# Attention kernel of two layers: both head groups averaged in one block, the row maxima turned in one 16-column turn, VectorE's and ScalarE's work put at other steps

## Chip, core, metric

One core of a Trainium2 chip. The metric is the device time of one execution in microseconds, lower is better.

## The reference, cut to what matters

Two layers of the same form run over x (128 rows of 256 tokens, 256 channels). Within a layer the rows are independent of each other; group norm needs all of them.

```python
def layer(x):                       # 128 rows x 256 tokens x 256 channels
    n = group_norm(x)
    q, k, v = heads(n @ Wq.T) * 32**-0.5, heads(n @ Wk.T), heads(n @ Wv.T)   # 8 heads of 32
    w = softmax(q @ k.T + bias + mask_bias)     # 256 x 256 for each row and head
    avg = sigmoid(n @ Wg.T + gate_bias) * (w @ v)
    return x + avg @ Wo.T + bo
```

## The kernel before

Each engine has one program: for each layer it goes through slots s = -2 to 132, one for each of the 128 rows and some to fill and drain; slots 8 to 123 are in a hardware loop of four slots a turn. In slot s the engines work on several rows at once: the projections are those of row s, the maxima those of row s-1, the exponentials of rows s-2 and s-3, the average of row s-3 or s-4, the output of row s-5. No planner decides anything: each engine executes its instructions in the order of the code, and an instruction whose semaphore isn't there holds all that stand behind it on its engine. TensorE and VectorE divide a slot into eight steps. In each step TensorE computes the logits of one head for the maxima (`max_bank`, two banks in turn) and of one head for the exponentials (`exp_bank`, two banks), and VectorE takes them: `maxima` (two halves, bias added, row maximum taken) and `logits` (bias added, written to `probs`).

Between these stands the rest. On TensorE before: step 0 `average(r, 1)` of row s-4; step 1 `maxima_rows`, the turn of the row maxima into `proj_b` (L757), and the q projection into `proj_a`; step 2 the k projection into `proj_b`; step 3 the output; step 4 the gate projection into `proj_b`; step 5 `average(r, 0)` of row s-3; steps 6 and 7 the v projection. `average` sums probabilities times v into `av_bank` (L739) and the sums of probabilities into `den_bank` (L746), in f32.

The row maxima are subtracted as two f16 rows of `q_stack`: ScalarE writes `coarse` (L463) from the turned maxima in `proj_b`, VectorE writes `fine` (L637) from `coarse` and `proj_b`, and SyncE sends both into the stack. The k projection writes over the same `proj_b`, so it waits for `fine`:

```python
if step == 2 and s.active():
    wait(pe, gate_ready, s.plus(-1).count(1, 1))
    wait(pe, fine_ready, s.plus(-2).count(1, 1))
    project(s, 1, pb, 0, None)
```

ScalarE's `split` takes a projection out of PSUM twice, as `k_hi` (f16, L444) and `k_f` (f32, L445); GpSimd makes `k_lo` of them; SyncE's queue sends, in this order, `coarse`, `fine`, `q_hi` twice, `k_hi` twice, `q_lo` and `k_lo` into the stacks, each when its semaphore is there. Step 0 of the next slot waits for all of them (`stack_in`), and the gate projection waits for `k_f`. VectorE's `gated_average`, `turn_denominator`, `invert` and `turn_reciprocal` prepare the gated, normalised average of row s-4.

Of the kernel before, what the change touches and what calls it, by code (L numbers as in the profile page):

```python
# [34 lines left out]
P = 128  # L35
# [78 lines left out]
def build(nc, a, out):  # L114
# [10 lines left out]
    with ctx:  # L125
# [71 lines left out]
        shift_ps = pb[0:HEADS, 0, :]  # L197
# [147 lines left out]
        def _(pool):  # L345
# [9 lines left out]
            def slot(s):  # L355
# [8 lines left out]
                if r.active():  # L364
                    key_sum(r, 0)
                if s.active():
                    low_half(s, 0)
                    low_half(s, 1)
                r = s.plus(-5)
                if r.active():  # L370
                    i = r.ring(2)
                    wait(pool, res_in[i], r.lap(2, 16, 16))
                    wait(pool, out_left, r.count(1, 1), pool_passed)
                    pool.tensor_tensor(y[:, i], y[:, i], attn[:, i], ALU.add).then_inc(y_ready, 1)  # L374
                r = s.plus(-4)
# [6 lines left out]
                r = s.plus(-3)  # L382
                if r.active():
                    key_sum(r, 1)
                r = s.plus(1)
                if r.active():
                    i = r.ring(2)
                    wait(pool, x_norm_ready, r.count(1, 1))
                    wait(pool, g_psum, r.plus(-2).count(1, 1))
                    wait(pool, v_psum, r.plus(-2).count(1, 1))  # L390
                    wait(pool, x_hi_ready, r.count(1, 1), pool_passed)
                    pool.tensor_tensor(x_lo[:, i], x_norm[:, i], x_hi[:, i], ALU.subtract).then_inc(x_lo_ready, 1)  # L392
# [10 lines left out]
            def key_sum(r, g):  # L403
                wait(pool, probs_ready, r.count(4, 2 * g + 2), pool_passed)
                wait(pool, den_psum, r.plus(-1).count(2, g + 1), pool_passed)
                pr = probs[:, r.ring(2), 4 * g:4 * (g + 1)]
                pool.tensor_tensor(probs_sum[:, g], pr[:, :, 0, :], pr[:, :, 1, :], ALU.add).then_inc(sum_ready, 1)  # L407
# [6 lines left out]
        def _(act):  # L414
# [32 lines left out]
            def slot(s):  # L447
# [9 lines left out]
                r = s.plus(-2)  # L457
                if r.active():
                    i = r.ring(2)
                    act.wait_ge(shift_psum, r.count(1, 1))  # L460
                    q = r.plus(-2)
                    wait(act, shift_in[q.ring(4)], shift_full(q))
                    act.activation(coarse[:, i], shift_ps, ACT.Copy, scale=-FINE / COARSE).then_inc(coarse_ready, 1)  # L463
# [10 lines left out]
                if s.active():  # L474
                    split(s, 0)
                    split(s, 1)
                r = s.plus(1)
                if r.active():
# [9 lines left out]
                    op.then_inc(x_norm_ready, 1)  # L488
                r = s.plus(-5)
# [8 lines left out]
                r = s.plus(-3)  # L498
                if r.active():
                    exponentials(r, 1, [0, 1])  # L500
# [9 lines left out]
                r = s.plus(1)  # L510
                if r.active():
                    i = r.ring(2)
                    act.wait_ge(x_norm_ready, r.count(1, 1))
                    wait(act, g_psum, r.plus(-2).count(1, 1))
                    wait(act, v_psum, r.plus(-2).count(1, 1))
                    act.activation(x_hi[:, i], x_norm[:, i], ACT.Copy).then_inc(x_hi_ready, 1)  # L516
# [5 lines left out]
                r = s.plus(-4)  # L522
                if r.active():
                    b = r.ring(2)
                    act.wait_ge(gated_ready, r.count(1, 1))
                    wait(act, out_psum, r.plus(-2).count(1, 1))
                    act.activation(gated_hi[:, b], gated[:, b], ACT.Copy).then_inc(gated_hi_ready, 1)  # L527
                if s.active():
                    act.wait_ge(v_psum, s.count(1, 1))
                    wait(act, av_psum, s.plus(-4).count(2, 2))  # L530
                    act.activation(v_sb[:, s.ring(4)], pa[:, :, :], ACT.Copy, scale=V_SCALE / W_SCALE).then_inc(v_ready, 1)  # L531
# [17 lines left out]
        def _(dve):  # L549
# [59 lines left out]
            def maxima(r, h):  # L609
# [6 lines left out]
                for t in range(TT):  # L616
# [3 lines left out]
                                                  op0=ALU.add, op1=ALU.max, accum_out=row_max[:, i, t, place(h):place(h) + 1])  # L620
                op.then_inc(max_done, 1)

            def logits(r, h):
# [3 lines left out]
                if h % 4 == 0:  # L627

                    wait(dve, av_psum, r.plus(-2).count(2, h // 4 + 1))
                    wait(dve, sum_ready, r.plus(-2).count(2, h // 4 + 1))  # L630
# [9 lines left out]
            def gated_average(r):  # L640
                dve.wait_ge(av_psum, r.count(2, 2))
# [5 lines left out]
            def turn_denominator(r):  # L647
                dve.wait_ge(den_psum, r.count(2, 2))
# [13 lines left out]
            def slot(s):  # L662
                l = s.layer
                for step in range(8):
                    if s.plus(-1).active():
                        maxima(s.plus(-1), step)
                    if step == 3 and s.plus(-4).active():
                        turn_denominator(s.plus(-4))
# [15 lines left out]
                    if step in (6, 7) and l == 0 and r.active():  # L684
                        dve.wait_ge(y_ready, r.count(1, 1))
                        c = step - 6
                        op = dve.bn_stats(stats[:, c, bass.ds(r.index(), 1), :], y[:, r.ring(2), c])  # L687
                        if c == CT - 1:
                            op.then_inc(stats_ready, 1)
# [7 lines left out]
        def _(pe):  # L697
# [33 lines left out]
            def average(r, g):  # L731
                pe.wait_ge(probs_ready, r.count(4, 2 * g + 2))
                pe.wait_ge(v_ready, r.count(1, 1))
                if g == 0:
                    wait(pe, avg_ready, r.plus(-1).count(1, 1))
                for t in range(TT):
                    for j in range(4):
                        h = 4 * g + j
                        op = pe.matmul(av_bank[HC * j:HC * (j + 1), g, :], v_sb[:, r.ring(4), t, HC * h:HC * (h + 1)],  # L739
                                       probs[:, r.ring(2), h, t, :], start=(t == 0), stop=(t == TT - 1))  # L740
                op.then_inc(av_psum, 1)
                pe.wait_ge(sum_ready, r.count(2, g + 1))
                if g == 0:
                    wait(pe, den_left, r.plus(-1).count(1, 1))
                for j in range(4):
                    op = pe.matmul(den_bank[HC * j:HC * (j + 1), g, :], ones[:, :], probs_sum[:, g, j, :],  # L746
                                   start=True, stop=True)
                op.then_inc(den_psum, 1)

            def maxima_rows(r):  # L750
# [5 lines left out]
                for t in range(TT):  # L756
                    op = pe.transpose(shift_ps[:, t * P:(t + 1) * P], row_max[:, i, t], ident[:, :])  # L757
                op.then_inc(shift_psum, 1)
# [12 lines left out]
            def slot(s):  # L771
                for step in range(8):
# [16 lines left out]
                    if step == 0 and r.active():  # L789
                        average(r, 1)  # L790
# [25 lines left out]
                    r = s.plus(-3)  # L816
                    if step == 5 and r.active():
                        average(r, 0)
# [63 lines left out]
```

## Time and profile before

| | |
|---|---|
| median of 3 runs | 3749.67 us (3744.16 to 3749.84) |
| the profiled execution | 3750.91 us, its span 3749.0 us |
| TensorE busy | 3495.1 us, 93% |
| VectorE busy | 3539.6 us, 94% |
| ScalarE, GpSimd busy | 73%, 81% |
| granted TensorE clock | 0.991 in the mean |

The span holds a prologue of some 150 us (the statistics of the input), the 128 rows of layer 0, a short boundary, and the 128 rows of layer 1. A busy share says how long an engine had an instruction in it, not which engine sets the pace; that is read from the waits and the chain.

### The profile page before, as it was taken

How to read it: one execution, taken by the hardware profiler on the slowest of the kernel's cores; microseconds unless marked ns; L12 is line 12 of the kernel's file. 1: busy time of each engine (PE TensorE's matmuls, PEld its weight loads, DVE VectorE, ACT ScalarE, POOL GpSimd, SP SyncE). 2: the span in 40 equal slices, each digit the busy share in tenths (PEclk: the TensorE clock that was granted, in tenths of full speed). 3: DMA queues.
4: the chain of work that ended last, by engine and by line, in shares of the span. 5: the costliest groups of instructions: out<-in, count | busy, mean ns of one | idle time of the engine just before them, and what ended most of it. 6: DMA issues, size and time to landing. Idle time of an engine off the chain costs nothing.

```text
span 3749.0 us, 121609 instructions
## 1 busy us (share of the span) xinstructions
PE 3495.1 (93%) x36360; PEld 2630.4 (70%) x36360; DVE 3539.6 (94%) x11937; ACT 2742.8 (73%) x4625; POOL 3021.8 (81%) x2056
## 2 busy tenths in 40 slices
PE   0499999999999999999968999999999999999997
PEld 0377777777777777777746777777777777777775
DVE  6599999999999999999968999999999999999997
ACT  0377777777777777777746777777787777777775
POOL 1288888888888888888856888888888888888887
PEclk9999999999999999999979999999999999999998
DMA  8555555555555555555534555555555555555553
GB/s 321 173 112 118 113 112 114 115 115 113 115 113 117 113 113 112 118 113 112 114 107 107 119 118 116 120 117 118 120 119 117 117 118 117 119 116 119 120 118 75
DMA packets 450644, 454.08 MB, mean 121 GB/s; under 512 B 42880, under 2 KB 445440, under 8 KB 445968
## 3 DMA queue, kind: packets, MB, share of 16 engines
q1 hardware_dynamic: 241680, 251.85, 35.5%
q10 hardware_dynamic: 208896, 201.38, 19.5%
q8 instruction: 37, 0.61, 0.1%
q14 instruction: 31, 0.25, 0.0%
HBM read 182.39 MB, written 67.24 MB: 67 GB/s over the span
## 4 chain that ended last, share of the span: by engine, by line
PE 58%; DVE 25%; issue 11%; DMA 3%; DVEq 1%; POOL 1%; SPq 1%; ACT 0%; POOLq 0%; ACTq 0%
PE proj_b L712 15%; DVE max_bank L618 10%; PE proj_a L712 9%; PE proj_a L766 9%; PE max_bank L723 8%; PE av_bank L739 7%; PE exp_bank L728 7%; DVE probs L631 6%; PE den_bank L746 3%; DVE row_max L618 3%; DVE stats L687 2%; DMA bias_k<-in_xT 1%; DVE recip L658 1%; DVE fine L637 1%; PE proj_b L757 1%
## 5 line engine op out<-in xcount | busy, mean ns | idle before, releaser
L618 DVE CUSTOM_DVE_ANT_0 max_bank<-max_bank,bias_q 128x256 f32<-128x256 f32 x4096 | 1637.6, 441 | 127.7 <-PE max_bank L723 95.7
L407 POOL TENSOR_TENSOR probs_sum<-probs 128x1024 f32<-128x1024 f32 x512 | 1207.8, 2359 | 308.3 <-ACT probs L434 154.3
L631 DVE TENSOR_TENSOR probs<-exp_bank,bias_k 128x512 f32<-128x512 f32 x2048 | 1390.0, 679 | 7.4 <-PE exp_bank L728 7.4
L723 PE MATMUL max_bank<-k_stack,q_stack 96*128 96x256 f16 (+1 forms) x4096 | 788.5, 274 | 11.8 <-DMA k_stack<-k_lo 9.9
L728 PE MATMUL exp_bank<-q_stack,k_stack 100*128 100x256 f16 x4096 | 784.4, 272 | 8.8 <-DVE probs L631 6.5
L431 ACT ACTIVATE probs<-probs,mask_bias 128x1024 f32<-128x1024 f32 x512 | 573.0, 1149 | 61.4 <-DVE probs L631 61.3
L434 ACT ACTIVATE probs<-probs 128x1024 f32<-128x1024 f32 x512 | 525.7, 1056 | 91.9 <-DVE probs L631 91.8
L618 DVE DVE_READ_ACCUMULATOR2_ANT row_max<- 128x1 f32 x4096 | 568.0, 139 | 0.0
L739 PE MATMUL av_bank<-probs,v_sb 128*32 128x256 f32 x8192 | 550.1, 386 | 3.0 <-ACT probs L431 1.6
L723 PEld LDWEIGHTS max_bank<-k_stack,q_stack 96*128 96x128 f16 (+1 forms) x4096 | 381.5, 98 | 164.0 <-DVE row_max L618 103.5
L728 PEld LDWEIGHTS exp_bank<-q_stack,k_stack 100*128 100x128 f16 x4096 | 395.1, 97 | 71.9 <-DVE probs L631 12.4
L392 POOL TENSOR_TENSOR x_lo<-x_norm,x_hi 128x512 f16<-128x512 f32 x256 | 299.0, 1168 | 147.0 <-ACT x_hi L516 147.0
L380 POOL TENSOR_TENSOR gated<-avg,recip 128x512 f32<-128x512 f32 x256 | 327.9, 1281 | 110.1 <-DVE recip L658 81.7
L374 POOL TENSOR_TENSOR y<-y,attn 128x512 f32<-128x512 f32 x256 | 327.1, 1278 | 101.1 <-ACT attn L495 65.3
L531 ACT ACTIVATE v_sb<-proj_a 128x512 f32<-128x512 f32 x256 | 152.9, 597 | 289.8 <-PE proj_a L712 289.8
L739 PEld LDWEIGHTS av_bank<-probs,v_sb 128*32 128x32 f32 x8192 | 214.0, 109 | 200.5 <-issue 57.6
L444 ACT ACTIVATE k_hi<-proj_b 128x512 f16<-128x512 f32 x256 | 152.8, 597 | 245.6 <-PE proj_b L712 245.6
L746 PE MATMUL den_bank<-probs_sum,ones 128*32 128x256 f32 x4096 | 317.7, 382 | 5.3 <-POOL probs_sum L407 5.3
L400 POOL TENSOR_TENSOR k_lo<-k_f,k_hi 128x512 f16<-128x512 f32 x256 | 296.9, 1160 | 29.5 <-issue 18.1
L400 POOL TENSOR_TENSOR q_lo<-q_f,q_hi 128x512 f16<-128x512 f32 x256 | 296.5, 1158 | 26.2 <-ACT q_f L445 26.2
L361 POOL TENSOR_TENSOR gated_lo<-gated,gated_hi 128x512 f16<-128x512 f32 x256 | 297.8, 1163 | 1.6 <-ACT gated_hi L527 1.6
L486 ACT ACTIVATE x_norm<-x_in,shift_x,rstd 128x256 f32<-128x256 f32 x512 | 278.5, 599 | 7.0 <-DMA x_in<-in_xT 6.8
(120 smaller groups left out, 6919.1 us busy)
## 6 DMA issues: line engine op xcount, KB each, us to landing
q_stack<-q_hi SPq DMA_DIRECT2D x512, 128.0 KB
k_stack<-k_hi SPq DMA_DIRECT2D x512, 128.0 KB
x_in<-in_xT ACTq DMA_DIRECT2D x128, 256.0 KB, 2.7
q_stack<-q_lo SPq DMA_DIRECT2D x256, 128.0 KB
k_stack<-k_lo SPq DMA_DIRECT2D x256, 128.0 KB
y<-in_xT ACTq DMA_DIRECT2D x128, 256.0 KB, 3.0
layer_out<-y ACTq DMA_DIRECT2D x128, 256.0 KB, 2.7
x_in<-layer_out ACTq DMA_DIRECT2D x128, 256.0 KB, 2.7
```

The costliest lines, as they stand in the source:

```text
L400: pool.tensor_tensor(qk_lo[m][:, b], qk_f32[m][:, b], qk_hi[m][:, b], ALU.subtract).then_inc(qk_lo_ready[m], 1)
L407: pool.tensor_tensor(probs_sum[:, g], pr[:, :, 0, :], pr[:, :, 1, :], ALU.add).then_inc(sum_ready, 1)
L431: act.activation(pr, pr, ACT.Exp, bias=mask_bias[:, bass.ds(r.index(), 1), t]).then_inc(probs_ready, 1)
L434: act.activation(pr, pr, ACT.Exp).then_inc(probs_ready, 1)
L618: op = dve.tensor_tensor_reduce(out=max_bank[h % 2][:, t, :], in0=max_bank[h % 2][:, t, :], in1=bias_q[:, h, t, :], scale=1.0 / FINE, scal ...
L631: dve.tensor_tensor(probs[:, r.ring(2), h], exp_bank[h % 2][:, :, :], bias_k[:, h], ALU.add).then_inc(logits_ready, 1)
L712: op = pe.matmul(ps[:, tile, :], lhs, rhs, start=(n == 0), stop=(n == len(terms) - 1))
L723: op = pe.matmul(bank_[:, t, :], q[0:n, t * P:(t + 1) * P], k[0:n, :], start=True, stop=True)
L728: op = pe.matmul(bank_[:, t, :], k[0:n, t * P:(t + 1) * P], q[0:n, :], start=True, stop=True)
L739: op = pe.matmul(av_bank[HC * j:HC * (j + 1), g, :], v_sb[:, r.ring(4), t, HC * h:HC * (h + 1)], probs[:, r.ring(2), h, t, :], start=(t == ...
L746: op = pe.matmul(den_bank[HC * j:HC * (j + 1), g, :], ones[:, :], probs_sum[:, g, j, :], start=True, stop=True)
L766: op = pe.matmul(pa[:, o, :], w[l][:, e, o * P:(o + 1) * P], g[:, b, e, :], start=(n == 0), stop=(n == len(terms) - 1))
```

## The change

Four things are put differently. TensorE averages both head groups in one block at step 0, both for row s-4, with the eight groups of `av_bank` first and the denominators behind them. The row maxima are stored as (head, half) so that one turn of 16 columns replaces two of 8; `coarse` and `fine` become 16 x 128 instead of 8 x 256. VectorE's `fine` moves from step 1 to step 2, the gated average from 2 to 4, the turn of the denominator and its reciprocal from 3 to 5, the turn of the reciprocal from 4 to 6, and both `bn_stats` to step 7. ScalarE's order is written anew: among others the first exponentials of the second head group now stand between the split of q and the split of k. GpSimd's order is written anew too.

```diff
-        row_max = sb("row_max", [P, 2, TT, HEADS], f32)
-        coarse = sb("coarse", [HEADS, 2, TOK], f16)
-        fine = sb("fine", [HEADS, 2, TOK], f16)
+        row_max = sb("row_max", [P, 2, HEADS, TT], f32)
+        coarse = sb("coarse", [HEADS * TT, 2, P], f16)
+        fine = sb("fine", [HEADS * TT, 2, P], f16)
-        shift_ps = pb[0:HEADS, 0, :]
+        shift_ps = pb[0:HEADS * TT, 0, 0:P]
...
                 if s.active():
                     split(s, 0)
-                    split(s, 1)
+                r = s.plus(-3)
+                if r.active():
+                    exponentials(r, 1, [0])
+                if s.active():
+                    split(s, 1)
+                r = s.plus(-3)
+                if r.active():
+                    exponentials(r, 1, [1])
...
-                r = s.plus(-3)
-                if r.active():
-                    exponentials(r, 1, [0, 1])
...
-                    if step == 3 and s.plus(-4).active():
+                    if step == 5 and s.plus(-4).active():
                         turn_denominator(s.plus(-4))
...
-                    if step == 1 and s.plus(-2).active():
+                    if step == 2 and s.plus(-2).active():
                         fine_shift(s.plus(-2))
...
-                        if step == 2:
+                        if step == 4:
                             gated_average(r)
-                        if step == 3:
+                        if step == 5:
                             invert(r)
-                        if step == 4:
+                        if step == 6:
                             turn_reciprocal(r)
...
+            def average(r):
+                pe.wait_ge(probs_ready, r.count(4, 4))
                 pe.wait_ge(v_ready, r.count(1, 1))
+                wait(pe, avg_ready, r.plus(-1).count(1, 1))
+                for g in range(HG):
+                    for t in range(TT):
+                        for j in range(4):
+                            h = 4 * g + j
+                            op = pe.matmul(av_bank[HC * j:HC * (j + 1), g, :],
...
+                op.then_inc(av_psum, 1)
+                wait(pe, den_left, r.plus(-1).count(1, 1))
+                for g in range(HG):
+                    pe.wait_ge(sum_ready, r.count(2, g + 1))
...
-                for t in range(TT):
-                    op = pe.transpose(shift_ps[:, t * P:(t + 1) * P], row_max[:, i, t], ident[:, :])
-                op.then_inc(shift_psum, 1)
+                pe.transpose(shift_ps, row_max[:, i].rearrange("p h t -> p (h t)"), ident[:, :]
+                             ).then_inc(shift_psum, 1)
...
                     if step == 0 and r.active():
-                        average(r, 1)
+                        average(r)
...
-                    if step == 5 and r.active():
-                        average(r, 0)
```

On VectorE, steps 1 and 2 of a slot before (the `ISA` rows are the two halves of `maxima`, L631 is `logits`):

```order
L618 ISA max_bank,row_max<-max_bank,bias_q 128x256 [waits max_psum]
L618 ISA row_max 128x1
L618 ISA max_bank,row_max<-max_bank,bias_q 128x256
L618 ISA row_max 128x1
L631 TENSOR_TENSOR probs<-exp_bank,bias_k 128x512 [waits exp_psum]
L637 SCALAR_TENSOR_TENSOR fine<-coarse,proj_b 8x256 [waits coarse_ready]
L618 ISA max_bank,row_max<-max_bank,bias_q 128x256 [waits max_psum]
```

And the same two steps of the changed kernel, in which each line number is one higher:

```order
L632 TENSOR_TENSOR probs<-exp_bank,bias_k 128x512 [waits exp_psum]
L619 ISA max_bank,row_max<-max_bank,bias_q 128x256 [waits max_psum]
L619 ISA row_max 128x1
L619 ISA max_bank,row_max<-max_bank,bias_q 128x256
L619 ISA row_max 128x1
L632 TENSOR_TENSOR probs<-exp_bank,bias_k 128x512 [waits exp_psum]
L638 SCALAR_TENSOR_TENSOR fine<-coarse,proj_b 16x128 [waits coarse_ready]
```

`fine` now stands behind the maxima and the logits of step 2, which wait for TensorE's matmuls of step 2.

On TensorE, step 0 and the start of step 1 before:

```order
L723 MATMUL max_bank<-k_stack,q_stack 128x256 [waits max_done,stack_in1]
L723 MATMUL max_bank<-k_stack,q_stack 128x256
L728 MATMUL exp_bank<-q_stack,k_stack 128x256 [waits logits_ready]
L728 MATMUL exp_bank<-q_stack,k_stack 128x256
L739 MATMUL av_bank<-probs,v_sb 32x256 [waits v_ready,probs_ready]
L739 MATMUL av_bank<-probs,v_sb 32x256 x7
L746 MATMUL den_bank<-probs_sum,ones 32x256 [waits sum_ready]
L746 MATMUL den_bank<-probs_sum,ones 32x256 x3
L757 MATMUL proj_b<-ident,row_max 8x128 [waits fine_ready,gate_ready,max_done]
L757 MATMUL proj_b<-ident,row_max 8x128
```

The same place in the changed kernel, and below the break the end of its step 2, where the k projection still waits for `fine_ready`:

```order
L739 MATMUL av_bank<-probs,v_sb 32x256 [waits avg_ready,v_ready,probs_ready]
L739 MATMUL av_bank<-probs,v_sb 32x256 x15
L747 MATMUL den_bank<-probs_sum,ones 32x256 [waits sum_ready,den_left]
L747 MATMUL den_bank<-probs_sum,ones 32x256 x3
L747 MATMUL den_bank<-probs_sum,ones 32x256 [waits sum_ready]
L747 MATMUL den_bank<-probs_sum,ones 32x256 x3
L757 MATMUL proj_b<-ident,row_max 16x128 [waits fine_ready,gate_ready,max_done]
...
L728 MATMUL exp_bank<-q_stack,k_stack 128x256
L712 MATMUL proj_b<-x_hi,w_hi0k 128x256 [waits fine_ready,gate_ready]
```

The block at step 0 holds twice the matmuls, the turn is one instruction, and what the k projection waits for is as it was.

On ScalarE, from the split of q to the second exponentials before (L434 is `exponentials`, L486 and L495 are x_norm and the output's bias):

```order
L444 ACTIVATE q_hi<-proj_a 128x512 [waits q_lo_ready,stack_in1,q_psum]
L445 ACTIVATE q_f<-proj_a 128x512
L444 ACTIVATE k_hi<-proj_b 128x512 [waits k_lo_ready,stack_in1,k_psum]
L445 ACTIVATE k_f<-proj_b 128x512
L486 ACTIVATE x_norm<-x_in,shift_x,rstd 128x256 [waits x_loaded0,x_lo_ready]
L486 ACTIVATE x_norm<-x_in,shift_x,rstd 128x256
L495 ACTIVATE attn<-proj_a,out_bias 128x256 [waits y_ready,out_psum]
L495 ACTIVATE attn<-proj_a,out_bias 128x256
L434 ACTIVATE probs<-probs 128x4x256 [waits logits_ready]
```

The same place in the changed kernel:

```order
L444 ACTIVATE q_hi<-proj_a 128x512 [waits q_lo_ready,stack_in1,q_psum]
L445 ACTIVATE q_f<-proj_a 128x512
L434 ACTIVATE probs<-probs 128x4x256 [waits logits_ready]
L444 ACTIVATE k_hi<-proj_b 128x512 [waits k_lo_ready,stack_in1,k_psum]
L445 ACTIVATE k_f<-proj_b 128x512
L434 ACTIVATE probs<-probs 128x4x256
```

The exponentials, which wait for VectorE's logits of step 3, now stand ahead of `k_hi` and `k_f`.

## Rows read from the trace of the kernel before

**Rows 1.** Page, part 1: busy time, share of the span, instructions of each engine.

```profile
PE 3495.1 (93%) x36360; PEld 2630.4 (70%) x36360; DVE 3539.6 (94%) x11937; ACT 2742.8 (73%) x4625; POOL 3021.8 (81%) x2056
```

**Rows 2.** Timeline, one slot of layer 0: start us, us, engine, what, [idle before].

```profile
1000.24 0.38 PE L757 MATMUL proj_b<-ident,row_max 128*8 128x128 f32 x2
...
1002.01 0.69 DVE L631 TENSOR_TENSOR probs<-exp_bank,bias_k 128x512 f32<-128x512 f32 x1
...
1002.61 0.40 DVE L637 SCALAR_TENSOR_TENSOR fine<-coarse,proj_b 8x256 f16<-8x256 f16 x1
...
1003.16 0.38 PE L712 MATMUL proj_b<-x_hi,w_hi0k 128*128 128x256 f16 x2 [0.34 <-DVE fine L637]
...
1004.46 0.38 PE L723 MATMUL max_bank<-k_stack,q_stack 96*128 96x256 f16 x2
...
1004.66 0.60 ACT L444 ACTIVATE k_hi<-proj_b 128x512 f16<-128x512 f32 x1 [1.17 <-PE proj_b L712]
...
1005.04 0.43 DVE L618 CUSTOM_DVE_ANT_0 max_bank<-max_bank,bias_q 128x256 f32<-128x256 f32 x1
...
1005.16 0.59 ACT L445 ACTIVATE k_f<-proj_b 128x512 f32<-128x512 f32 x1
...
1005.37 1.19 SPq L326 DMA_DIRECT2D k_stack<-k_hi  x2
...
1005.77 0.71 DVE L649 STREAM_TRANSPOSE den_turned<-den_bank 128x512 f32<-128x512 f32 x1
...
1007.37 0.55 SPq L326 DMA_DIRECT2D k_stack<-k_lo  x1
...
1009.07 0.40 DVE L618 CUSTOM_DVE_ANT_0 max_bank<-max_bank,bias_q 128x256 f32<-128x256 f32 x1
...
1012.14 0.38 PE L723 MATMUL max_bank<-k_stack,q_stack 96*128 96x256 f16 x2
...
1014.10 0.09 PEld L757 LDWEIGHTS proj_b<-ident,row_max 128*8 128x8 f32 x2 [0.41 <-issue]
```

**Rows 3.** Critical chain in order of time, layer 1: start us, us, what.

```profile
2603.38 1.31 PE proj_b L712 x12
...
2605.13 1.00 PE av_bank L739 x16
2606.13 0.43 PE den_bank L746 x8
2606.56 0.33 PE max_bank L723 x2
...
2610.74 0.31 PE proj_b L757 x2
...
2624.29 0.31 PE proj_b L757 x2
```

**Rows 4.** Groups by line: busy us, mean ns of one, idle before.

```profile
L431 ACT ACTIVATE probs<-probs,mask_bias 128x1024 f32<-128x1024 f32 x512 | 573.0, 1149 | 61.4 <-DVE probs L631 61.3
...
L434 ACT ACTIVATE probs<-probs 128x1024 f32<-128x1024 f32 x512 | 525.7, 1056 | 91.9 <-DVE probs L631 91.8
...
L687 DVE BATCH_NORM_STATS2 stats<-y 128x256 f32 (+1 forms) x256 | 106.2, 416 | 11.7 <-POOL y L374 11.7
L637 DVE SCALAR_TENSOR_TENSOR fine<-coarse,proj_b 8x256 f16<-8x256 f16 x256 | 102.0, 398 | 0.0
...
L599 DVE TENSOR_TENSOR centred<-centred 128x2 f32<-128x2 f32 x2 | 0.3, 160 | 0.0
```

**Rows 5.** Timeline, where PE waited for the last stack transfer: start of layer 0.

```profile
156.46 0.60 SPq L326 DMA_DIRECT2D k_stack<-k_lo  x1
...
160.03 0.39 PE L723 MATMUL max_bank<-k_stack,q_stack 96*128 96x256 f16 x2 [1.21 <-DMA k_stack<-k_lo]
```

**Rows 6.** Critical chain in order of time, layer 0: start us, us, what.

```profile
1016.56 0.33 DVE fine L637
```

**Rows 7.** Windows between the layers: busy of each engine, PEclk is the granted clock.

```profile
1940.00:1945.00 5.00, 2.48 (x12) 1.66 (x12) 0.00 (x0) 0.63 (x1) 1.57 (x2) 0.50 0.15 52
1970.00:1975.00 5.00, 2.79 (x24) 2.27 (x24) 0.00 (x0) 3.12 (x7) 2.31 (x2) 1.00 0.65 140
```

More of the change, by code:

```diff
@@ L456, in slot @@
                     act.dma_start(x_in[:, i], channel_major(src[l], r.index() * TOK, TOK)).then_inc(x_loaded[i], 16)
-                r = s.plus(-2)
+                r = s.plus(-5)
                 if r.active():
[L459 to L463, printed above, removed]
+                    b = r.ring(2)
+                    act.wait_ge(gated_ready, r.count(1, 1))
+                    wait(act, out_psum, r.plus(-2).count(1, 1))
+                    act.activation(gated_hi[:, b], gated[:, b], ACT.Copy).then_inc(gated_hi_ready, 1)
                 r = s.plus(-3)
@@ L473, in slot @@
                     act.dma_start(y[:, i], channel_major(src[l], r.index() * TOK, TOK)).then_inc(res_in[i], 16)
-                if s.active():
-                    split(s, 0)
-                    split(s, 1)
+                r = s.plus(-2)
+                if r.active():
+                    i = r.ring(2)
+                    act.wait_ge(shift_psum, r.count(1, 1))
+                    q = r.plus(-2)
+                    wait(act, shift_in[q.ring(4)], shift_full(q))
+                    act.activation(coarse[:, i], shift_ps, ACT.Copy, scale=-FINE / COARSE).then_inc(coarse_ready, 1)
                 r = s.plus(1)
@@ L488, in slot @@
                     op.then_inc(x_norm_ready, 1)
+                    act.wait_ge(x_norm_ready, r.count(1, 1))
+                    wait(act, g_psum, r.plus(-2).count(1, 1))
+                    wait(act, v_psum, r.plus(-2).count(1, 1))
+                    act.activation(x_hi[:, i], x_norm[:, i], ACT.Copy).then_inc(x_hi_ready, 1)
+                if s.active():
+                    split(s, 0)
+                r = s.plus(-3)
+                if r.active():
+                    exponentials(r, 1, [0])
+                if s.active():
+                    split(s, 1)
+                r = s.plus(-3)
+                if r.active():
+                    exponentials(r, 1, [1])
                 r = s.plus(-5)
@@ L627, in logits @@
                 if h % 4 == 0:
-                    wait(dve, av_psum, r.plus(-2).count(2, h // 4 + 1))
+                    wait(dve, av_psum, r.plus(-2).count(1, 1))
                     wait(dve, sum_ready, r.plus(-2).count(2, h // 4 + 1))
@@ L676, in slot @@
                     if r.active():
[L677 removed]
+                        if step == 4:
                             gated_average(r)
[L679 removed]
+                        if step == 5:
                             invert(r)
[L681 removed]
+                        if step == 6:
                             turn_reciprocal(r)
                     r = s.plus(-5)
[L684 removed]
+                    if step == 7 and l == 0 and r.active():
                         dve.wait_ge(y_ready, r.count(1, 1))
[L686 to L689, printed above, removed]
+                        for c in range(CT):
+                            op = dve.bn_stats(stats[:, c, bass.ds(r.index(), 1), :], y[:, r.ring(2), c])
+                        op.then_inc(stats_ready, 1)
             for l in range(2):
```

62 lines of the change are left out of this document (17 added, 45 removed).

## Prediction

> **What bounds the kernel now.** I read the page first: VectorE is busy 94% and TensorE 93% of the span [rows 1], so neither busy share settles it, and a change that makes one wait for the other has no spare time to hide in. Then I read the timeline of one slot. The reader is to see two turns of the row maxima, 13.86 us apart (1014.10 - 1000.24) [rows 2]: that is a slot in layer 0. In layer 1 the chain in order of time has them 13.55 us apart (2624.29 - 2610.74), and its pieces join end to end on TensorE [rows 3]. With 128 rows a layer the slots are 128 x (13.86 + 13.55) = 3508 us of the span; the rest is prologue and boundary. So the question is how long one slot takes afterwards.
>
> The coupling that matters is small at present. The k projection waits for `fine`, and TensorE loses 0.34 us by it: `fine` starts at 1002.61, takes 0.40, and the projection starts 0.15 after its end, at 1003.16 [rows 2]. It is that little because VectorE does `fine` after the logits of step 1, while TensorE still has a whole q projection ahead of its step 2.
>
> **What the change saves.** A block of eight groups and their denominators is 1.00 + 0.43 us, and the maxima behind it take 0.33, where 1.31 for twelve matmuls says that two should take 0.22 [rows 3]. Since 8 denominator instructions are 0.43, the 16 others should be 0.86: 0.14 goes into entering the block and 0.11 into leaving it. One block in place of two saves 0.25 us of TensorE, one turn in place of two 0.10 (half of 0.31 less the 0.11 for leaving). On VectorE `fine` goes from 398 ns at 256 elements towards the 160 ns of an operation of 2 elements; in proportion 128 elements take 0.28 us. The bounds are 0.16 and 0.40 [rows 4]. I take 0.28. If nothing new had to be waited for, the slot would shorten by 0.12 us in layer 0 (VectorE) and by 0.35 in layer 1 (TensorE), 60 us in all.
>
> **What it adds: three legs, walked through from step 0.** I put t = 0 at TensorE's first matmul of step 0, layer 0.
>
> TensorE: maxima and exponentials' logits 0.44; the merged block 2 x 1.43 - 0.14 = 2.72, so 3.16; leaving it and one turn 0.21, so 3.37; the logits of step 1 0.44, the q projection 1.31; step 2 starts at 5.12 [rows 3].
>
> VectorE starts a head's maxima 0.58 us after TensorE's first matmul for it (1004.46 to 1005.04), needs 0.73 for them (to 1005.77), and starts what follows the logits 0.60 behind their start (1002.01 to 1002.61) [rows 2]. So the maxima of step 2 start at 5.70, the logits at 6.43, `fine` at 7.03, it ends at 7.31, and the k projection starts at 7.46. TensorE was ready at 5.56: it now stands 1.9 us, since nothing but those logits lies between what VectorE needs and what it holds back. That is the first new stall. The range of `fine` moves it by 0.12 at most.
>
> The k projection takes 1.30 (1003.16 to 1004.46) [rows 2]; step 3 starts at 8.76, VectorE's maxima at 9.34, its logits at 10.07, done 0.69 later at 10.76. Only then can ScalarE start the exponentials that now stand ahead of the split of k: 10.86 with 0.1 to hand over, as SyncE takes between the end of `k_hi` (1005.26) and its issue at 1005.37. They take 1.06 [rows 4] of which the next instruction overlaps 0.1, as `k_f` starts 0.50 into a `k_hi` of 0.60 [rows 2]: `k_hi` starts at 11.81 and ends at 12.41. Before, it followed its projection at once. `k_f` ends at 12.90 (start 0.50 later, 0.59 long), and the gate projection, ready at 8.76 + 0.44 + 1.31 + 0.44 = 10.95, waits for it until 13.0: the second new stall, 2.0 us.
>
> SyncE issues `k_hi` at 12.52 and, 2.00 later as before (1005.37 to 1007.37), `k_lo` at 14.52 [rows 2]. Where TensorE was seen to wait for this transfer, it started 3.57 us after the issue (156.46 to 160.03) [rows 5]; in the steady part it needed no wait 4.77 us after it (1007.37 to 1012.14) [rows 2], which is the bound from above. I take 3.7, near the one that shows the landing. Then step 0 of the next slot starts at 18.2. TensorE, with 1.31 + 3 x 0.44 + 2 x 0.66 behind 13.0, is ready at 16.95: the third stall, 1.3 us. In layer 1 the exponentials are 0.09 longer (1149 against 1056 ns) [rows 4]: 18.3.
>
> The Trainium skill ("DMA: Bandwidth & Descriptors", section "Anatomy of one DMA") fits one DMA of the GpSimd path with a fixed 2.0 us and its bytes over 436 GB/s. By that the last 128 KB would be there 2.3 us after issue, at an estimated 16.8, and the transfer would not bind; the trace shows 3.57 us with five others ahead of it, so the sum goes by the trace.
>
> The sum: 128 x (18.2 - 13.86) = 555 and 128 x (18.3 - 13.55) = 608, together 1163 us on the profiled 3750.91, which is within 0.04% of the median of 3749.67: 4914, and I say **4910 us**. VectorE's moved turns and ScalarE's other moves cost nothing beside this: both engines stand for several microseconds a slot. That cover is thin on VectorE in layer 0 only, next.
>
> **The rivals.**
>
> *The transfer does not bind (0.13).* Then the loop closes through an engine. TensorE's gives 16.95 and 17.05. VectorE's: maxima of step 5 start at 13.0 + 1.31 + 0.58 = 14.9; before, from those maxima (1009.07) to the next `fine` (1016.56) it took 7.49 [rows 2, 6]; now two turns (0.71 each [rows 2], less an overlap of 0.08 as others have), the reciprocal (0.16, that of the smallest operation [rows 4]) and step 2's maxima and logits (1.33) stand in that stretch too, while some 0.2 of waiting for TensorE may drop out. `fine` comes at 24.9 against 7.03, a slot of 17.9. In layer 1 it goes without the two `bn_stats` (0.42 each [rows 4], less the overlap) and waits 0.1 longer for ScalarE, 17.3. Time: 3751 + 128 x (4.04 + 3.75) = 4750. For it speaks that transfers find less traffic in a longer slot; against it, that 3.57 was seen in the thin traffic of the first slots.
>
> *The transfer lands late (0.06).* With the full 4.77 a slot is 1.07 longer: 3751 + 1163 + 274 = 5190. `coarse` and `fine` are twice as many packets of half the size; they have 2 us of room before step 4 needs them.
>
> *Only one stall comes (0.04).* If ScalarE found the logits of step 3 done, k would leave PSUM at once and only the wait for `fine` stayed: TensorE's 13.4 us of a slot before (13.55 less some 0.2 for `fine`), less 0.35, plus 1.9 is 14.9, so 4060 us. It decides if VectorE runs a step ahead of TensorE; but its logits need TensorE's step 3.
>
> *The clock falls (0.03).* TensorE works 13 of 18.2 us, with gaps of 1.3 to 2 us. Between the layers the granted clock was 0.50, the 1.2 GHz level, in 5 us in which TensorE was busy for 2.48, and 1.00, 2.4 GHz, in 5 us with 2.79 [rows 7]. At the low level the parts of the loop on TensorE, 5.12 + 1.30, would double: 24.6 and 24.7 a slot, 3751 + 128 x (10.8 + 11.1) = 6550. The Trainium skill ("TensorE: Matmul & The Clock Gate", section "HAM oscillation — how this bites in real kernels") describes kernels in which waits between bursts bring the clock down each time; the row at 1.00 with 2.79 busy, less than TensorE has in every stretch of the new slot but the longest gap, speaks against it here.
>
> *Faster (0.02).* If TensorE kept its pace past `fine`, the savings alone would remain: 3751 - 60 = 3690. That needs `fine` done by t = 5.56 rather than 7.31. The point from which the change is a gain is a loop below 13.86: all three stalls, 5.2 us together, would have to shrink to 0.5.
>
> **How the numbers follow.** My case (0.72) has its own range of 4800 to 5020: hand-overs of 0.1 us and the landing by -0.3 to +0.4 us, 256 times. The range of 8 in 10 takes in rival one and part of the late landing: 4700 to 5060. A change within 0.2% is about what a measurement of this kernel cannot tell from none: every case but the last is slower by far (0.98); I leave 0.01 of it for no change: faster 0.02, same 0.01, slower 0.97.
>
> **What the profile will show.** The turns (L757) 18.2 and 18.3 us apart; TensorE's waits for `fine` before the k projection near 1.9 us, for `k_f` before the gate projection near 2 us, for the stack's transfer near 1.3 us, each some 250 times; ScalarE idle before the first exponentials of group 1, `k_hi` right behind them. TensorE's busy share falls to about 70%; `fine` takes some 280 ns. I am wrong if the k projection starts less than 1.5 us behind step 2's logits, if `k_hi` does not follow an exponential, or if the clock is below 0.97.

## The result and the profile after

The changed kernel takes 4987.35 us (median, 4966.6 to 4993.02), beside 3749.47 for the kernel before on the same chip: a ratio of 1.3296 [1.3265, 1.3326]. 4910 was forecast, so it is inside the range and 77 us above the number. The profiled execution took 4993.02 us with a span of 4990.5.

The page of the kernel after, part 1, and two rows of its part 5, answer to [rows 1, 4]:

```profile
PE 3730.6 (75%) x36104; PEld 2667.7 (53%) x36104; DVE 3543.4 (71%) x11937; ACT 2714.5 (54%) x4625; POOL 3020.0 (61%) x2056
...
L431 ACT ACTIVATE probs<-probs,mask_bias 128x1024 f32<-128x1024 f32 x512 | 585.3, 1144 | 633.6 <-DVE probs L632 633.6
L434 ACT ACTIVATE probs<-probs 128x1024 f32<-128x1024 f32 x512 | 538.7, 1053 | 655.4 <-DVE probs L632 655.4
```

VectorE's and ScalarE's busy times are those of before to within 30 us; both only wait more. TensorE has 256 matmuls fewer and is busy for 236 us more. a_fine1 below does the same matmuls at a clock of 0.990 and is busy for 3581.7 us, so about 150 of the 236 us go with the lower clock here; the rest was not taken apart. The exponentials now have 634 and 655 us of idle time ahead of them where [rows 4] had 61 and 92: ScalarE comes to them before the logits exist.

The view of the waits of the kernel after (who waits, for whom; us in total, times, longest):

```profile
PE proj_b L712 <- ACT k_f L445: 474.9, 256, 3.0
PE proj_b L712 <- DVE fine L638: 424.6, 252, 2.0
...
PEld exp_bank L728 <- DVE probs L632: 258.9, 466, 1.7
...
PE exp_bank L728 <- DVE probs L632: 135.2, 270, 1.4
...
PE max_bank L723 <- DMA k_stack<-k_lo: 15.7, 24, 2.4
```

Two of the three forecast stalls are there with the forecast count. The third is not: the stack's transfer is named 24 times, and `exp_bank` waiting for VectorE's logits some 270 times stands in its place. The transfer is not out of the loop, though: in the chain that ended last (part 4 of the page, shares of the span) it has 8%.

```profile
PE proj_b L712 14%; PE av_bank L739 10%; PE proj_a L712 8%; DMA k_stack<-k_lo 8%; DVE max_bank L619 8%; DVE probs L632 7%; PE max_bank L723 6%; PE den_bank L747 4%; PE exp_bank L728 4%; ACT k_hi L444 3%; DVE row_max L619 3%; ACT k_f L445 2%; POOL k_lo L400 1%; DVE den_turned L650 1%; PE proj_b L757 1%
```

The timeline of one slot of layer 0 (idle time before in brackets) shows all of it, and answers to [rows 2]:

```profile
1008.41 0.28 PE L757 MATMUL proj_b<-ident,row_max 128*16 128x128 f32 x1
...
1010.28 0.38 PE L723 MATMUL max_bank<-k_stack,q_stack 96*128 96x256 f16 x2
...
1011.58 0.68 DVE L632 TENSOR_TENSOR probs<-exp_bank,bias_k 128x512 f32<-128x512 f32 x1
...
1012.19 0.27 DVE L638 SCALAR_TENSOR_TENSOR fine<-coarse,proj_b 16x128 f16<-16x128 f16 x1
...
1012.51 0.39 PE L712 MATMUL proj_b<-x_hi,w_hi0k 128*128 128x256 f16 x2 [1.63 <-DVE fine L638]
...
1015.13 0.68 DVE L632 TENSOR_TENSOR probs<-exp_bank,bias_k 128x512 f32<-128x512 f32 x1
...
1015.94 1.06 ACT L434 ACTIVATE probs<-probs 128x1024 f32<-128x1024 f32 x1 [3.30 <-DVE probs L632]
...
1016.90 0.58 ACT L444 ACTIVATE k_hi<-proj_b 128x512 f16<-128x512 f32 x1
...
1018.02 0.39 PE L712 MATMUL proj_b<-x_hi,w_hi0g 128*128 128x256 f16 x2 [1.83 <-ACT k_f L445]
...
1019.58 0.55 SPq L326 DMA_DIRECT2D k_stack<-k_lo  x1
...
1020.65 0.71 DVE L650 STREAM_TRANSPOSE den_turned<-den_bank 128x512 f32<-128x512 f32 x1
...
1020.88 0.38 PE L723 MATMUL max_bank<-k_stack,q_stack 96*128 96x256 f16 x2
...
1021.29 0.65 DVE L632 TENSOR_TENSOR probs<-exp_bank,bias_k 128x512 f32<-128x512 f32 x1
...
1022.00 0.39 PE L728 MATMUL exp_bank<-q_stack,k_stack 100*128 100x256 f16 x2 [0.73 <-DVE probs L632]
...
1023.15 0.39 PE L723 MATMUL max_bank<-k_stack,q_stack 96*128 96x256 f16 x2
...
1023.46 0.11 PEld L728 LDWEIGHTS exp_bank<-q_stack,k_stack 100*128 100x128 f16 x2 [0.20 <-DVE probs L632]
```

- `fine` lasts 0.27 us and stands behind the logits of step 2; the k projection stands 1.63 us.
- ScalarE waits 3.30 us for the logits of step 3, does an exponential, and only then `k_hi`. The gate projection stands 1.83 us.
- From the issue of `k_lo` (1019.58) to step 0 (1023.15) it is 3.57 us, the very figure of [rows 5]. Yet TensorE had already lost time in step 7: its logits started at 1022.00, 0.90 after the maxima's two matmuls (0.22) were through, because VectorE turned the denominator before it did the logits of step 5. Only 0.26 is lost at 1023.15 (the projection's last pair starts at 1022.67 and takes 0.22), and the weight load for the next logits still waits for VectorE at 1023.46. So two legs end together at step 0. The maxima wait for the transfer, as I read it: VectorE had left their bank 0.29 before (1022.86), and in a_qlo below, where the transfer leaves earlier, TensorE starts 0.05 behind VectorE there (1002.71 to 1002.76). The logits, 0.31 later, wait for VectorE. In 226 of 228 steady slots TensorE's logits of step 0 start within 0.1 us of the end of VectorE's logits of step 6.

In the chain this turn is at 1008.48 and the next at 1026.58, 18.10 us on. At full clock the slots are 18.18 us in layer 0 and 18.26 in layer 1, where 18.2 and 18.3 were forecast. But not all slots have the full clock. The windows of the kernel after put two gate projections side by side, the first starting at 998.74 and the second at 1018.02 (length; busy of PE, PEld, DVE, ACT, POOL; granted clock; DMA share, GB/s):

```profile
995.60:999.10 3.50, 1.66 (x16) 1.24 (x15) 2.94 (x10) 2.45 (x4) 0.05 (x1) 0.99 0.13 40
999.10:1002.50 3.40, 3.40 (x19) 2.34 (x17) 0.68 (x3) 2.09 (x5) 3.09 (x3) 0.50 0.76 154
1002.50:1006.00 3.50, 3.09 (x30) 1.92 (x32) 3.50 (x12) 0.60 (x1) 1.59 (x1) 1.00 0.22 76
1014.90:1018.40 3.50, 1.67 (x16) 1.25 (x15) 2.93 (x9) 2.46 (x4) 0.07 (x1) 1.00 0.15 43
1018.40:1021.80 3.40, 2.86 (x27) 2.23 (x24) 1.88 (x6) 2.06 (x5) 3.09 (x3) 1.00 0.75 154
```

TensorE did the same before both, 1.66 and 1.67 us of work in 3.5. Behind the first the granted clock is 0.50, the 1.2 GHz level, for 3.4 us and TensorE is busy all of it; behind the second it stays at 1.00, 2.4 GHz. Of 114 steady slots of layer 0 that I went through 48 have such a stretch, in layer 1 55 of 115, and such a slot takes 19.1 to 19.2 us. Each stretch begins 0.07 to 1.27 us behind the gate projection's start, in this kernel never at the k projection. 103 slots by about 0.95 us are some 98 us.

### The profile page after: what moved, and what is told of

Same layout as the page of the kernel before. It is cut to its first block, busy times and chain, and to the rows that moved or that the text cites. A ratio compares the mean times of both kernels' runs of the same rounds, so it can differ in the third digit from the quotient of the medians.

```text
span 4990.5 us, 119942 instructions
## 1 busy us (share of the span) xinstructions
PE 3730.6 (75%) x36104; PEld 2667.7 (53%) x36104; DVE 3543.4 (71%) x11937; ACT 2714.5 (54%) x4625; POOL 3020.0 (61%) x2056
## 4 chain that ended last, share of the span: by engine, by line
PE 48%; DVE 22%; issue 12%; DMA 9%; ACT 6%; POOL 2%; SPq 1%; DVEq 1%; ACTq 0%; POOLq 0%
PE proj_b L712 14%; PE av_bank L739 10%; PE proj_a L712 8%; DMA k_stack<-k_lo 8%; DVE max_bank L619 8%; DVE probs L632 7%; PE max_bank L723 6%; PE den_bank L747 4%; PE exp_bank L728 4%; ACT k_hi L444 3%; DVE row_max L619 3%; ACT k_f L445 2%; POOL k_lo L400 1%; DVE den_turned L650 1%; PE proj_b L757 1%
## 5 line engine op out<-in xcount | busy, mean ns | idle before, releaser
L728 PE MATMUL exp_bank<-q_stack,k_stack 100*128 100x256 f16 x4096 | 836.8, 288 | 146.1 <-DVE probs L632 135.2
L431 ACT ACTIVATE probs<-probs,mask_bias 128x1024 f32<-128x1024 f32 x512 | 585.3, 1144 | 633.6 <-DVE probs L632 633.6
L434 ACT ACTIVATE probs<-probs 128x1024 f32<-128x1024 f32 x512 | 538.7, 1053 | 655.4 <-DVE probs L632 655.4
L723 PE MATMUL max_bank<-k_stack,q_stack 96*128 96x256 f16 (+1 forms) x4096 | 840.1, 289 | 32.2 <-DMA k_stack<-k_lo 15.7
L728 PEld LDWEIGHTS exp_bank<-q_stack,k_stack 100*128 100x128 f16 x4096 | 378.9, 102 | 334.1 <-DVE probs L632 258.9
L739 PE MATMUL av_bank<-probs,v_sb 128*32 128x256 f32 x8192 | 503.4, 387 | 3.2 <-ACT probs L431 1.7
L723 PEld LDWEIGHTS max_bank<-k_stack,q_stack 96*128 96x128 f16 (+1 forms) x4096 | 398.9, 104 | 160.1 <-DVE row_max L619 58.8
L739 PEld LDWEIGHTS av_bank<-probs,v_sb 128*32 128x32 f32 x8192 | 242.3, 111 | 194.1 <-issue 61.0
L712 PE MATMUL proj_b<-x_hi,w_hi1g 128*128 128x256 f16 x512 | 109.6, 299 | 245.0 <-ACT k_f L445 245.0
L712 PE MATMUL proj_b<-x_hi,w_hi0g 128*128 128x256 f16 x512 | 110.6, 302 | 229.9 <-ACT k_f L445 229.9
```

The source lines that it names most:

```text
L431: act.activation(pr, pr, ACT.Exp, bias=mask_bias[:, bass.ds(r.index(), 1), t]).then_inc(probs_ready, 1)
L434: act.activation(pr, pr, ACT.Exp).then_inc(probs_ready, 1)
L712: op = pe.matmul(ps[:, tile, :], lhs, rhs, start=(n == 0), stop=(n == len(terms) - 1))
L723: op = pe.matmul(bank_[:, t, :], q[0:n, t * P:(t + 1) * P], k[0:n, :], start=True, stop=True)
L728: op = pe.matmul(bank_[:, t, :], k[0:n, t * P:(t + 1) * P], q[0:n, :], start=True, stop=True)
```

## The experiments

**One part undone at a time.** Three kernels from the one after: `fine` at step 1 again; the split of k ahead of the exponentials again; both.

```
a_fine1:   -  if step == 2 and s.plus(-2).active():      # fine_shift
           +  if step == 1 and s.plus(-2).active():
a_ksplit:  -  split(s, 0); exponentials(r, 1, [0]); split(s, 1); exponentials(r, 1, [1])
           +  split(s, 0); split(s, 1); exponentials(r, 1, [0, 1])
a_both:    both edits
```

> The changed kernel with one line put back: VectorE's fine at step 1 again. My theory (each stall is a leg of one loop): TensorE's stall before the k projection (1.63 us in the profile after) goes, everything behind it comes earlier, a slot falls from 18.2 to about 16.5 us, the time to about 4500 us (4450 to 4560). Rival (ScalarE's order or the merged block alone sets the pace, and fine only fills a gap that is there anyway): the time stays above 4900 us.

Measured: 4447.97 us (one execution), 2 below the range, clock 0.990, slots of 16.44 us in layer 0 and 16.51 in layer 1.

> The changed kernel with ScalarE's split of k put back ahead of the exponentials of group 1; all else as changed. My theory: k_hi follows its projection at once, TensorE's stall before the gate projection (1.83 us) goes, and the stack's last transfer leaves some 2 us earlier; a slot of 16.2 to 16.5 us, 4400 to 4500 us. Rival (the wait for fine alone sets the pace): above 4900 us.

Measured: 4413.82 us (one execution), clock 0.990, slots of 16.32 us in both layers.

> The changed kernel with both put back, fine at step 1 and the split of k ahead of the exponentials. If the two waits are all that is wrong, what the change saves should show: 13.4 us a slot, about 3690 us. My theory now is that it does not get there: ScalarE still does x_norm and x_hi ahead of the split of q, so the stack's transfers leave late, and the block of 48 matmuls keeps VectorE waiting: 15.0 to 15.2 us a slot, about 4110 us (4000 to 4200).

Measured: 4036.20 us (one execution), clock 0.991, slots of 14.69 and 14.98, in the range though the slots are shorter than expected.

The waits of the three kernels, in this order, show that each edit takes away its own stall and leaves the other as it was (in the last two the lines of the code stand four lower):

```profile
PE proj_b L712 <- ACT k_f L445: 411.7, 255, 3.0
```

```profile
PE proj_b L708 <- DVE fine L634: 424.8, 252, 2.0
```

```profile
PE proj_b L708 <- ACT k_f L445: 5.4, 9, 1.2
```

So the two stalls are shown, each caused by its own edit. Each kernel is 539 and 574 us faster than the kernel after. In both figures the low clock goes too (92 us, below), so they can't be added: with both stalls gone it is 951 us. The remaining 287 us over the kernel before belong to what is left in a_both: the merged block, the turn, VectorE's moved steps and ScalarE's and GpSimd's other moves. My sum had the block inside TensorE's leg (2.72 us) and put no price on the rest.

**The same parts made alone in the kernel before.**

```
b_fine2:      -  if step == 1 and s.plus(-2).active():   # fine_shift
              +  if step == 2 and s.plus(-2).active():
b_exp_first:  -  split(s, 0); split(s, 1); exponentials(r, 1, [0, 1])
              +  split(s, 0); exponentials(r, 1, [0]); split(s, 1); exponentials(r, 1, [1])
b_merge:      -  average(r, 1) at step 0, average(r, 0) at step 5
              +  average(r) at step 0: both groups' matmuls, then both groups' denominators
b_turn16:     -  row_max [P, 2, TT, HEADS];  two transposes, of row_max[:, i, t]
              +  row_max [P, 2, HEADS, TT];  one transpose, of row_max[:, i] as "p (h t)"
              -  coarse, fine [HEADS, 2, TOK]
              +  coarse, fine [HEADS * TT, 2, P]
```

> The kernel before with one thing of the change alone: VectorE's fine at step 2. My theory: the k projection must wait for the logits of step 2 here as well, 1.5 to 1.7 us more a slot on TensorE: 15.1 to 15.4 us, 4080 to 4180 us. Rival (only behind the merged block is TensorE at step 2 so early that it must wait): below 3800 us.

Measured: 4169.94 us (one execution; before on the same chip 3746.96), clock 0.991, slots of 15.36, as expected. Eight of its steady slots (5 of layer 0, 3 of layer 1) take some 17.0 us and have a stretch of 3.4 us at 0.50. Here it begins at the k projection, 0.9 to 1.1 us behind its start and behind 1.85 us of idle time. A window of b_fine2 behind the k projection that starts at 267.67 (columns as above):

```profile
268.60:271.90 3.30, 3.30 (x17) 2.29 (x16) 1.69 (x6) 2.06 (x4) 1.12 (x2) 0.50 0.32 105
```

> The kernel before with one thing of the change alone: ScalarE's first exponentials of group 1 ahead of the split of k. My theory: k_hi comes some 2 us later, which TensorE waits for before the gate projection and again for the stacks at step 0: 16.3 to 16.5 us a slot, 4400 to 4450 us. Rival (in the old order the exponentials' logits are done in time): below 3800 us.

Measured: 4595.32 us (one execution), 145 to 195 more than expected, and the clock says why: 0.949. Its slots are 16.47 and 16.31 us at full clock and 17.97 and 17.82 with a stretch at 0.50, which 46 of 114 and 58 of 115 have. Those 104 by 1.5 us are 156: without them about 4440, as expected. The waits of b_exp_first:

```profile
PE proj_b L716 <- ACT k_f L445: 630.2, 256, 3.7
```

That is 2.46 us each time, the longest regular wait of any kernel here, and it stands at the gate projection again.

> The kernel before with one thing of the change alone: both groups averaged in one block of 48 matmuls at step 0, VectorE, ScalarE and GpSimd in their old order. By the entering and leaving that it saves on TensorE (0.25 us a slot) it should give 3690 to 3750 us. My theory is that VectorE waits 2.8 us for the next maxima behind the block and that this is not made up: about 14.4 us a slot, 3900 to 3960 us.

Measured: 3920.55 us (one execution), slots of 14.40 and 14.38. The merged block, which by the prediction's estimate TensorE does 0.25 us faster than two, costs 174 us in the old order. The timeline of b_merge shows the reason:

```profile
1001.45 1.93 PE L739 MATMUL av_bank<-probs,v_sb 128*32 128x256 f32 x32
...
1003.68 0.69 DVE L631 TENSOR_TENSOR probs<-exp_bank,bias_k 128x512 f32<-128x512 f32 x1
...
1004.39 0.38 PE L723 MATMUL max_bank<-k_stack,q_stack 96*128 96x256 f16 x2
...
1004.97 0.43 DVE L618 CUSTOM_DVE_ANT_0 max_bank<-max_bank,bias_q 128x256 f32<-128x256 f32 x1 [0.60 <-PE max_bank L723]
```

For the 2.7 us of the block TensorE hands VectorE nothing, VectorE runs dry: it waits for the maxima's matmuls for 287.3 us over the run, 268 times, where the kernel before has 95.7 us, 147 times. These 192 us more are about what the kernel loses. That a VectorE that was 94% busy [rows 1] can't make them up later, while two blocks of half the length find it with work left, is my reading; no run varies the length of the block.

> The kernel before with one part of the change alone: row_max as (head, half), one turn of 16 columns, coarse and fine as 16 x 128. My theory: fine takes 0.27 instead of 0.40 us on VectorE, ScalarE's coarse 0.1 less, TensorE has one turn less (0.11): a slot shorter by 0.12 to 0.15 us in layer 0 and 0.15 to 0.25 in layer 1, together 3700 to 3720 us, a ratio of 0.988 to 0.992. Rival (the stacks' 256-byte pieces land later, or another engine has the pace): 3750 us or more.

Measured: 3703.62 us (median of four executions, 3702.65 to 3708.18), ratio 0.9884 [0.9868, 0.9901], slots of 13.71 and 13.37. This one part of the change is a gain, of 44.5 us or 1.2%, and this kernel beats both. Its groups by line, against 398 ns in [rows 4] for the same values laid out 8 x 256:

```profile
L637 DVE SCALAR_TENSOR_TENSOR fine<-coarse,proj_b 16x128 f16<-16x128 f16 x256 | 67.9, 265 | 0.0
```

`coarse` on ScalarE goes from 361 to 251 ns in the same way. The values are as many; only those of one partition are half as many, and the time falls with them.

**The clock.** Useless work for TensorE in one gap or the other, in scratch space that the program overwrites before it reads it.

```
a_fill:      step 2, ahead of the wait for fine:
             +  for n in range(12): pe.matmul(pb[64:128, 1, :], 64x256 ...)
a_fill_out:  step 3, ahead of output(r, 0):
             +  for n in range(12): pe.matmul(pa[:, n % 2, :], 128x256 ...)
```

> The changed kernel with twelve matmuls without use (64 x 256, f16, 0.109 us each, 1.31 us in all) on TensorE in step 2 ahead of the wait for fine, into a part of proj_b that the k projection writes over afterwards. They fit into the stall of 1.63 us, so the loop stays as long as it was. Theory of the clock: in the profile after, some 4 slots in 10 have 3.4 us at the 1.2 GHz level and are 19.2 instead of 18.2 us; with the longest gap filled TensorE keeps 2.4 GHz, and the time falls by about 0.4 x 256 x 1.0 = 100 us to some 4880. Rival (the low clock has nothing to do with how much TensorE does in that gap, or the slots are long for another reason): 4960 us or more.

Measured: 4962.66 us (median of four, 4961.06 to 4964.92), ratio 1.3246 [1.3224, 1.3268], clock 0.958. TensorE's idle time at `fine` goes from 424.6 to 48.4 us, and still 48 and 49 slots have the low stretch. The theory missed and its rival held: the gap at step 2 is not the one.

> The changed kernel with twelve matmuls without use (128 x 256, f16, 0.109 us each, 1.31 us in all) on TensorE in step 3, ahead of the output projection and into the bank that it writes over. They take their time out of TensorE's gap of 1.83 us before the gate projection, at which every stretch of low clock begins in the profile after; the first filling, in the gap at step 2, changed nothing. Theory of this gap: with it down to some 0.5 us the granted clock goes back to 0.99, the 19.2 us slots vanish, the time falls by about 0.45 x 256 x 0.95 = 110 us to 4880 (4860 to 4920). Rival (the clock falls by the sum of the gaps or by chance): 4950 us or more at a clock of 0.95 to 0.96.

Measured: 4895.71 us (median of four, 4893.47 to 4897.41), ratio 1.3062 [1.304, 1.3084]. The gap ahead of the gate projection shrinks to 0.53 us, as the waits and the timeline of a_fill_out show,

```profile
PE proj_b L712 <- ACT k_f L445: 151.3, 256, 2.9
```

```profile
1016.43 0.39 PE L712 MATMUL proj_b<-x_hi,w_hi0g 128*128 128x256 f16 x2 [0.53 <-ACT k_f L445]
```

and no steady slot of it has a low stretch; the slots are 18.19 and 18.27 us, what the kernel after has at full clock, and the clock over the span is 0.992.

So 3072 matmuls that nobody needs make the kernel 92 us faster (4987 to 4896). That is what the low clock costs, close to the 98 counted above.

**What closes the loop.** SyncE issues the four stack transfers in the order q_hi, q_lo, k_hi, k_lo, so that k_lo has less ahead of it; and, with that, VectorE turns the denominator behind the logits of step 5 in place of ahead of them.

```
a_qlo:      -  for m, part in ((0, hi), (1, hi), (0, lo), (1, lo))
            +  for m, part in ((0, hi), (0, lo), (1, hi), (1, lo))
a_qlo_den:  as a_qlo, and
            -  step 5: turn_denominator, logits, invert
            +  step 5: logits, turn_denominator;  step 6: logits, invert
```

> The changed kernel with q_lo sent ahead of the two k_hi on SyncE's queue, so that three transfers in place of four stand at the end and k_lo leaves 0.7 us earlier. Theory one, that the stack's last transfer alone closes the loop as I predicted: a slot loses 0.3 to 0.7 us, 4820 to 4910 us. Theory two, that VectorE's turn of the denominator ahead of the logits of step 5 holds TensorE in step 7 and is only 0.1 to 0.3 us from the transfer: 4930 to 4970 us.

Measured: 4974.19 us (median of four, 4970.35 to 4983.09, which overlaps the kernel after's 4966.6 to 4993.02), ratio 1.3276 [1.3253, 1.3298]; slots at full clock 18.20 and 18.26, unchanged. The transfer has left the chain, in which all DMAs together have 2% of the span, and `k_lo` is used 3.33 us behind its issue (999.43 to 1002.76) with no wait for it. So the transfer alone doesn't close the loop. The timeline of a_qlo at step 0 shows who does:

```profile
1002.57 0.68 DVE L632 TENSOR_TENSOR probs<-exp_bank,bias_k 128x512 f32<-128x512 f32 x1
...
1003.30 0.11 PEld L728 LDWEIGHTS exp_bank<-q_stack,k_stack 100*128 100x128 f16 x2 [0.43 <-DVE probs L632]
```

TensorE's logits of step 0 need the bank that VectorE's logits of step 6 leave.

> The same, and the turn of the denominator after the logits of step 5 instead of ahead of them (the reciprocal at step 6 ahead of the turn of the reciprocal). By theory two both legs that end at step 0 now come earlier and this is clearly faster than the one before: another 0.1 to 0.3 us a slot, 4860 to 4930 us. By theory one it is the same as with q_lo alone.

Measured: 4923.56 us (median of four, 4918.78 to 4928.75), ratio 1.3131 [1.3109, 1.3153]; slots at full clock 18.04 and 18.13. TensorE's stall in step 7 shrinks from 0.90 to 0.30 us (counted as above), but the 0.71 us of the turn buy only 0.16 and 0.13 a slot over a_qlo (some 37 us; most of the other 14 goes with fewer low stretches, 40 and 46). The timeline of a_qlo_den says why: the turn still stands ahead of the logits of step 6, and for those step 0 waits as before.

```profile
1009.52 0.55 SPq L326 DMA_DIRECT2D k_stack<-k_lo  x1
...
1011.19 0.70 DVE L650 STREAM_TRANSPOSE den_turned<-den_bank 128x512 f32<-128x512 f32 x1
...
1012.51 0.68 DVE L632 TENSOR_TENSOR probs<-exp_bank,bias_k 128x512 f32<-128x512 f32 x1
...
1013.25 0.11 PEld L728 LDWEIGHTS exp_bank<-q_stack,k_stack 100*128 100x128 f16 x2 [0.43 <-DVE probs L632]
```

Here step 0's logits come 3.74 us behind the issue of `k_lo` (1009.52 to 1013.26), in the kernel after 3.88 (1019.58 to 1023.46): 0.14 less, which is the gain.

## Why the prediction was right, and where it was not

**The two new stalls: right, and sized.** "The k projection starts at 7.46" was 7.55 behind TensorE's first matmul of step 0 (1023.15 to 1030.70 in the chain). There "it now stands 1.9 us" was 1.63 us of idle time, and 1.79 when a pair of matmuls is counted as 0.22 us, as the prediction does. "The second new stall, 2.0 us" was 1.83, and 2.00 counted so. `fine` at 0.28 took 0.27. a_fine1 and a_ksplit take each away alone; b_fine2 and b_exp_first make each alone. The rival of one stall only is excluded by the waits of the kernel after, which have both; and a_ksplit, which has the one that it kept, takes 4414 us and not its 4060.

**The third stall: right in size, in its cause only half.** I wrote "step 0 of the next slot starts at 18.2" by the landing of `k_lo`, and TensorE "ready at 16.95". That transfer does hold step 0's maxima in part of the slots (8% of the chain; in a_fill_out, where no slot is stretched by the clock, 13%). But a second leg is as long, and that the sum came out with one of the two left out was luck: they end within some tenths of a us of each other. TensorE was not ready: 0.90 of the 1.3 us were lost before, in step 7. The step that failed is VectorE's leg under "the transfer does not bind", 17.9 and 17.3. It followed VectorE round to its own next `fine`, and did not ask where TensorE waits for VectorE's logits on that way: at step 7 for those of step 5, at step 0 for those of step 6, and the merged block of 2.7 us comes behind. With the transfer moved forward the slots stay at 18.20 and 18.26 (a_qlo), so this leg is 18.2 in both layers, not 17.9 and 17.3. How much of a slot the transfer would still hold with VectorE's leg shortened was not settled.

**The clock: the term that was missing.** The sum had none for it, and gave 0.03 to a rival in which the clock falls in every slot (6550). Its own sign of being wrong, a clock below 0.97, came: 0.953. The clock fell in 103 of 229 slots, each time for about 3.4 us; half of 3.4 is 1.7 us of TensorE's work, of which some 0.95 reached the slot. Slots alone give 128 x (18.18 - 13.85) + 128 x (18.26 - 13.61) = 1149 us where my sum had 1163; with the clock's 92 the difference is 1241, and 1238 were measured. The slots of before in this are the mean over the steady slots, not the two that I read (13.61 in layer 1 for 13.55). So the 77 us by which the forecast is low are the clock's 92 less some 14 of a sum that was slightly high. [rows 7] with 1.00 at 2.79 busy of 5 us I took as evidence against a fall; it was a row of one moment between the layers, and the pair of windows above shows that the busy time before a gap doesn't tell what follows. The section of the Trainium skill that I weighed it against ("TensorE: Matmul & The Clock Gate", "HAM oscillation — how this bites in real kernels") has waits between bursts bring the clock down again and again: the trace agrees in kind, at 1.83 us of idle time in 103 slots of 229, where a_fill_out with 0.53 has none.

**"VectorE's moved turns and ScalarE's other moves cost nothing beside this": right beside the stalls, not by itself.** Under 5 us of stalls they are hidden. Without them a_both stays 287 us above the kernel before, where my "faster" rival put it at 3690. b_merge has 174 for the block alone, in the old order; that it costs as much in the new one is not shown. The rest, with the turn's gain of 44.5 to be added, wasn't taken apart; in a_both `k_lo` is issued at 1015.50, step 0 starts at 1019.22, 3.7 us later, and `k_lo` has 13% of the chain, so the transfer may well bind there. The faster case needed more than `fine` in time; "one block in place of two saves 0.25 us of TensorE" was true and not worth having, and of the "60 us in all" only the turn's 44.5 were measured as a gain. That "all three stalls, 5.2 us together, would have to shrink to 0.5" holds for layer 1 (18.3 - 5.2 = 13.1 against 13.55); for the 13.86 named there it would be 0.9.

## What to carry to other kernels

When a step is moved on one engine, find the matmuls that its input comes from and the matmuls that its result holds back; if both stand in the same step of the loop, the whole latency between two engines is bare in every turn (1.63 and 1.83 us here, 256 times). Walk each leg of a loop with both engines' waits in it, not one engine's work, since the leg that closes it changes engine. Bundling work on one engine can starve the one that feeds on it (192 us more of VectorE's waits here). Of a change in several parts, try each alone, as the one that was a gain (0.9884) was buried under the others.

## What was not expected of the hardware

- In the kernel after the granted clock fell to 0.50 for about 3.4 us in some 45% of the slots, always from the gate projection on, behind 1.83 us idle, and never at the k projection behind 1.63. In a_fine1, with a mean of 1.6 us at the gate projection (411.7 / 255), no slot had it. b_fine2 shows that the place alone doesn't decide: 8 of its 229 steady slots fell, at the k projection, behind 1.85 us. Work put into the gap gave 92 us back.
- With the same busy time before (1.66 and 1.67 us of 3.5) one slot fell and the next did not; what chose between them is open.
- TensorE used the 128 KB of `k_lo` 3.57 us behind their issue in the kernel after and 3.58 in a_fill_out (1018.00 to 1021.58), as in [rows 5], though in the first two VectorE's work was due within 0.3 us of it. With `q_lo` sent earlier 3.33 us were enough (a_qlo). The agreement misled me as much as it confirmed the sum.
